# A two-layer conditioned attention kernel: in the second layer, one GpSimd chain for both normalizations, and the second film's input turned by VectorE and block loads

## The reference: what is computed

```
# layer 0
xn = layer_norm(x); q, k, v = xn @ Wq + bq, xn @ Wk + bk, (xn @ Wv + bv) * mask
y  = softmax(q k^T + mask term) v
h  = layer_norm(y) * (1 + scale(emb)) + shift(emb)         # "film"
x  = x + silu(h) @ out_w + out_b
# layer 1
xn = layernorm(x); q, k, v = ...; k = -inf and v = 0 where masked
q  = softmax(q over the 16 features); k = softmax(k over time)
y  = q @ (k^T v)                                           # linear attention per head
h  = layernorm(y) * (1 + scale(emb)) + shift(emb)
out = x + silu(h) @ film_out_W + film_out_b
```

## Time and profile before

| what | us |
|---|---|
| median of 3 runs | 890.01 (888.34 to 890.52) |
| the profiled execution, its own time | 891.08 |
| its span, first to last instruction | 889.1 |
| busy in the span: PE, DVE, ACT, POOL | 856.3, 780.8, 671.3, 615.6 |
| busy in 600 to 800 us: PE, DVE, ACT, POOL (of 200) | 200.00, 181.47, 178.34, 178.65 |

### The profile page before, as it was taken

How to read it: one execution, slowest core, us unless ns; L and a number is a source line. 1 busy time by engine, 2 the same in 40 slices (tenths; PEclk the granted TensorE clock), 3 DMA queues, 4 the chain that set the end, 5 groups by cost and what they waited for, 6 DMA issues and landing times.

```text
span 889.1 us, 23631 instructions
## 1 busy us (share of the span) xinstructions
PE 856.3 (96%) x8304; PEld 707.8 (80%) x8304; DVE 780.8 (88%) x1609; ACT 671.3 (76%) x1200; POOL 615.6 (69%) x1095
## 2 busy tenths in 40 slices
...
GB/s 257 261 191 110 176 124 166 135 147 152 139 151 146 152 128 172 114 183 118 173 116 162 99 44 113 61 83 84 85 84 84 84 84 86 95 94 90 50 31 60
DMA packets 91237, 108.55 MB, mean 122 GB/s; under 512 B 8624, under 2 KB 61328, under 8 KB 90992
## 3 DMA queue, kind: packets, MB, share of 16 engines
...
...
## 4 chain that ended last, share of the span: by engine, by line
PE 89%; DVE 3%; issue 3%; POOL 2%; ACT 1%; SPq 0%; DMA 0%; DVEq 0%; ACTq 0%; POOLq 0%
PE psX L1447 16%; PE psY L1568 13%; PE psT L1447 10%; PE psM L1447 10%; PE psT L1547 6%; PE psT L1526 5%; PE psY L1447 5%; PE psY L1593 3%; PE psM L1547 3%; PE psT L1458 3%; PE psT L1725 3%; PE psY L1678 3%; PE psM L1526 3%; PE psX L1605 2%; PE psM L1458 1%
## 5 line engine op out<-in xcount | busy, mean ns | idle before, releaser
L1037 DVE TENSOR_REDUCE sb_cm<-psT 128x4 f32<-128x1024 f32 x168 | 202.6, 1217 | 11.9 <-PE psT L1547 11.7
L618 ACT ACTIVATE sb_P<-psT 128x1024 f32<-128x1024 f32 x176 | 177.7, 1025 | 29.4 <-PE psT L1526 15.1
L1568 PE MATMUL psY<-sb_P,sb_Vp 128*17 128x256 f32 x2048 | 130.2, 383 | 1.8 <-DVE sb_yr L1063 1.2
L1037 DVE TENSOR_REDUCE sb_cm<-psM 128x4 f32<-128x1024 f32 x88 | 107.1, 1217 | 7.5 <-PE psM L1547 7.4
L418 POOL TENSOR_SCALAR sb_ve<-sb_mv 128x2 f32<-128x2 f32 x32 | 7.3, 229 | 125.0 <-DVE sb_mv L1071 124.9
L1447 PE MATMUL psX<-sb_xT,sb_W0h 128*128 128x256 f32 x488 | 93.6, 294 | 0.0
L618 ACT ACTIVATE sb_P<-psM 128x1024 f32<-128x1024 f32 x80 | 81.9, 1024 | 12.9 <-PE psM L1526 6.8
L1568 PEld LDWEIGHTS psY<-sb_P,sb_Vp 128*17 128x17 f32 x2048 | 50.3, 97 | 48.1 <-issue 5.4
L436 POOL TENSOR_TENSOR sb_qp<-sb_qp 128x512 fp32r<-128x512 f32 x64 | 82.1, 1283 | 5.3
L1547 PE MATMUL psT<-sb_Ks,sb_Qs 64*128 64x256 f32 x672 | 74.7, 304 | 2.7 <-DVE sb_cm L1037 1.4
L1526 PE MATMUL psT<-sb_Qs,sb_Ks 64*128 64x256 f32 x704 | 74.5, 296 | 2.4 <-ACT sb_P L618 2.2
...
## 6 DMA issues: line engine op xcount, KB each, us to landing
...
sb_u<-y_normed SPq DMA_DIRECT2D x128, 64.0 KB, 2.5
...
```

The lines of the kernel that those rows point to most:

```text
L618: a.activation(P[G % 4][:, :], pairs[place["S", n, g][0]][:, :], ACT.Exp).then_inc(s_ex, 1)
L1037: v.tensor_reduce(cm[n % 2][:, 4 * j:4 * j + 4], scores, AX.X, ALU.max, negate=True).then_inc(s_mx, 1)
L1568: ins = pe.matmul(psY[32 * j:32 * j + 17, y0:y0 + T], Vp[n % RING][:, m, 4 * gr + j, :], Pj[:, c0:c0 + 256], start=(m == 0), stop=(m == 1))
```

## The change

Four edits, all in the second stage:

1. `rs_pair(n)` takes the place of `rs_(n, 0)` and of `rs_(n-3, 1)` for n = 3 to 31: one chain of four instructions on four columns. It waits for the statistics of both, so for `st0_`[n] and `st1_`[n-3], and both `xn_`[n] and `yn_`[n-3] wait for it.
2. The low part of the first film's result (`hl_`) for samples 4 to 31 goes from DVE to POOL as `hl0_`, behind `xb_`.
3. For the 27 samples 0 to 26 (`BLOCKS`), `f1_` on PE is gone. A new `ynt_`[t-4] on DVE makes the 32x32 block transposes of `yn`, SyncE stores the result to a new DRAM tensor `y_second` (`fstore`) and reads it back in four block loads (`fload`), and ACT's `u_` of the second film reads that SBUF tile in the next turn, ahead of `t_`[t-5]. `o0_` no longer waits for that `u_`.
4. Order: on DVE `mq_` goes ahead of `bd_`; on ACT `hh_`[t] goes ahead of `yn_`; in the ramp `yt_`(1), (2) and (3) stand earlier.

```diff
+PAIRED = range(3, B)
+BLOCKS = B - 5
...
+        def scaled(n, l):
+            first = n if l == 0 else n + 3
+            if first in PAIRED:
+                return e_rsp, 4 * (first - 2)
+            return (e_rs0, 4 * n + 4) if l == 0 else (e_rs1, 4 * (n - B + 3) + 4)
...
+            def fstore(n):
+                sp.wait_ge(e_f1, n + 1)
+                sp.dma_start(fd[n], y1s.rearrange("p a e -> p (a e)")).then_inc(e_fd, 16)
+
+            def fload(n):
+                sp.wait_ge(e_fd, 16 * n + 16)
+                if n >= 2:
+                    sp.wait_ge(e_u1, n - 1)
+                by_block = fd[n].rearrange("(b s) (a e) -> a s b e", s=32, a=4)
+                tile = y1T[n % 2].rearrange("p b i k s -> p b (i k s)")
+                for q in range(4):
+                    sp.dma_start(tile[32 * q:32 * q + 32, :, :], by_block[q]).then_inc(e_fl[n % 2], 16)
...
                 if ok(t - 1):
                     key_mask(t - 1)
+                if 0 <= t - 4 < BLOCKS:
+                    fstore(t - 4)
+                    fload(t - 4)
...
+            def rs_pair(n):
+                done, count = scaled(n, 0)
+                g.wait_ge(e_st0, 4 * n + 4)
+                g.wait_ge(e_st1, 4 * (n - 3) + 4)
+                g.wait_ge(e_xn, n)
+                if n >= 4:
+                    g.wait_ge(e_yn, n - 3)
+                g.tensor_scalar(ve[:, :], mv[:, :, 1], EPS, None, ALU.add).then_inc(done, 1)
+                g.wait_ge(done, count - 3)
+                g.tensor_tensor(rs[:, :], ve[:, :], ph[:, :], ALU.pow).then_inc(done, 1)
+                g.wait_ge(done, count - 2)
+                g.tensor_tensor(ve[:, :], mv[:, :, 0], rs[:, :], ALU.mult).then_inc(done, 1)
+                g.wait_ge(done, count - 1)
+                g.tensor_scalar(nm[:, :], ve[:, :], -1.0, None, ALU.mult).then_inc(done, 1)
...
+            def hl0_(n):
+                g.wait_ge(e_hh0, n + 1)
...
+                g.tensor_tensor(hl[0][n % 2].bitcast(F32R), hb[0][n % 2], hh[0][n % 2], ALU.subtract).then_inc(e_hlp, 1)
...
             def yn_(n):
-                a.wait_ge(e_rs1, 4 * n + 4)
+                a.wait_ge(*scaled(n, 1))
...
+            def ynt_(n):
+
+                v.wait_ge(e_yn, n + 1)
+                if n >= 1:
+                    v.wait_ge(e_fd, 16 * n)
+                v.transpose(y1s.rearrange("p a (i k s) -> p k i a s", i=2, k=2),
+                            yn[n % 2].rearrange("p k (i a c) -> p k i a c", i=2, a=4)).then_inc(e_f1, 1)
...
                 if ok(t + 1):
                     yt_(t + 1)
+                if 0 <= t - 4 < BLOCKS:
+                    ynt_(t - 4)
                 if ok(t - 2):
                     dq_(t - 2)
+                    mq_(t - 2)
                 if ok(t - 3):
                     bd_(t - 3)
-                if ok(t - 2):
-                    mq_(t - 2)
-                if ok(t):
-                    hl_(t)
                 if ok(t - 6):
                     ob_(t - 6)
...
-                if ok(t - 4):
+                if t - 4 >= BLOCKS:
                     f1_(t - 4)
```

More of the change, by code:

```diff
@@ L192, in bass_cond_seq_kernel @@
         ub[1], th[1], hb[1], hh[1], hl[1] = ([unit() for _ in range(2)] for _ in range(5))
+        y1s = unit().rearrange("p k (b s) -> p (k b) s", k=2, b=2)
+        y1T = [unit().rearrange("p k (b i s) -> p (k b) i s", k=2, b=2, i=2)
+               .rearrange("p a i (k s) -> p a i k s", k=2) for _ in range(2)]
         R = [psT[0][:, 0:512], psT[0][:, 512:1024], psT[1][:, 0:512], psT[1][:, 512:1024],
@@ L236, in bass_cond_seq_kernel @@
         e_hlast = sem("e_hlast")
+        e_rsp, e_hlp = sem("e_rsp"), sem("e_hlp")
+        e_fd = sem("e_fd")
+        e_fl = [sem(f"e_fl{i}") for i in range(2)]
         e_xb, e_xo, e_rs0, e_rs1, e_qs = (sem(f"e_{n}") for n in ("xb", "xo", "rs0", "rs1", "qs"))
@@ L475, in rs_ @@
                 k = slice(2 * l, 2 * l + 2)
+                done, count = scaled(n, l)
                 g.wait_ge(e_st[l], 4 * n + 4)
@@ L529, in second @@
                 if ok(t - 1):
-                    rs_(t - 1, 0, e_xn)
+                    rs_pair(t - 1)
                 if ok(t):
                     xb_(t)
+                if ok(t):
+                    hl0_(t)
                 if ok(t - 2):
@@ L586, in _ @@
             kb_(B - 2)
-            rs_(B - 1, 0, e_xn)
+            rs_pair(B - 1)
             ken_(B - 2)
@@ L654, in u_ @@
             def u_(n, l, src):
-                a.wait_ge(e_f[l], n + 1)
+                if l == 1 and n < BLOCKS:
+                    a.wait_ge(e_fl[n % 2], landed(n, 2, 4))
+                else:
+                    a.wait_ge(e_f[l], n + 1)
                 if n == 0:
@@ L660, in u_ @@
                 for d in range(2):
-                    ins = a.activation(ub[l][n % 2][:, d, :], src[:, d, :], ACT.Identity,
-                                       bias=FB[:, l, d, n:n + 1], scale=FA[:, l, d, n:n + 1])
+                    dst, blocks = ub[l][n % 2][:, d, :], src[:, d, :]
+                    if l == 1 and n < BLOCKS:
+                        dst = dst.rearrange("p (k b s) -> p b k s", k=2, b=4)
+                        blocks = y1T[n % 2][:, :, d, :, :]
+                    ins = a.activation(dst, blocks, ACT.Identity, bias=FB[:, l, d, n:n + 1],
+                                       scale=FA[:, l, d, n:n + 1])
                 ins.then_inc(e_u[l], 1)
@@ L671, in xn_ @@
             def xn_(n):
-                a.wait_ge(e_rs0, 4 * n + 4)
+                a.wait_ge(*scaled(n, 0))
                 if n >= 1:
@@ L741, in second @@
                 if ok(t - 5):
+                    if t - 5 < BLOCKS:
+                        u_(t - 5, 1, r_f1)
                     t_(t - 5, 1)
```

51 lines of the change are left out of this document (26 added, 25 removed).

## The result

The changed kernel takes 909.38 us (median of 4 runs, 908.52 to 913.01) against 890.26 of before on the same chip: a ratio of 1.0239, with a 95% interval of 1.0214 to 1.0263. It is slower. The profiled execution took 909.97 us with a span of 908.2.

A forecast was written before the change was run, and what follows sets the result against it. PE's own work bounded the kernel at 10.71 us a turn; a new ring of waits would make it 11.46, +20.3 us over 27 turns. With +0.2 for the rest: 911.6 profiled, 910.5 against the median, range 894 to 922.

The forecast's parts named there:

- The ring: Second stage, once per turn: `st0_`, pair, `yn_`, `ynt_`, `dq_`, `mq_`, `bd_`, `y_`, `yd_`; summed at 11.46 us against 10.71.
- PE's wait ahead of `y_`: Sign in the changed profile: PE waits 0.7 to 1.2 us before `y_`, released by DVE's `bd_`.
- DVE's ahead of `ynt_`: Sign in the changed profile: DVE waits about 1 us before `ynt_`, released by ACT's `yn_`.
- C: Length of the paired chain on four columns on POOL: 2.22 us held, 1.87 free.
- the line through one and two columns: POOL's power took 0.57 us on one column, 0.71 on two; extended straight, 0.99 on four.
- the hold: POOL's multiply in the pair, starting beside DVE's second `h_`, is held until that ends; C 2.22 instead of 1.87.
- PE's 0.44: PE loses `f1_`, 0.44 us per turn: 10.71 to 10.27 if nothing else binds.
- The low part on POOL: `hl0_`, estimated at 1.3 us on POOL; DVE's sum stays, and any delay of `kt_` hides behind PE's slack.
- rival 2: Ring of `yn_`, `ynt_`, store, loads and ACT: summed at 10.4 us; slower DMA makes 12.0, 925 us; chance 0.13 with long power.
- The rest: Outside the steady turns: ramp -0.7 us from ACT's wait, tail +1 from `yn_`[28]; taken as +0.2 together, good to 2.
- PE before 540 us unchanged: Sign in the changed profile: PE's work ahead of 540 us, in the ramp, stays as before.

## Why the prediction was right

**The ring.** It was made from ten rows of the kernel before, and came out as predicted: 11.46 summed, 11.48 to 11.49 measured; +20.3 over 27 turns summed, +20.33 measured from `y_`[1] to `y_`[28] (the steady turns are 0.78 longer, the last of them only 0.13). PE's wait ahead of `y_` (0.92) and DVE's ahead of `ynt_` (0.92) are where they were said to be.

**C.** Summed 2.22, measured 715.09 - 712.85 = 2.24. The power on four columns takes 1.04; the line through one and two columns gave 0.99. The multiply takes 0.48, held until the end of the second `h_`; undoing the hold alone gave 0.26 a turn, so the step stands on a run and not only on an overlap in the timeline.

**PE's 0.44.** It is worth nothing here: PE waits in every turn. Nor does any version show the 10.27 in a steady turn; the shortest take 10.5. The low part on POOL was costed as neutral, since DVE's sum stays. That was the wrong reading of it. Back on DVE behind `bd_` it costs 13 us, because its place beside `qs_` holds it, so in the changed kernel it is worth 0.44 us a turn. It is also a member of the second ring, which costs 0.36 a turn once the first is gone; 0.15 of that came back when it left.

**The ring of store and loads** (rival 2) was summed at 10.4 and thought harmless. In the changed kernel it is: store to first load 2.03 us, ACT waits 0.5 us in all. The two versions with `ynt_` behind `mq_` show it at about 10.5 with late landings on top, so it stood 1 us behind, about as summed, and kept them at 892.8 and 888.7.

**The rest** was mis-sized in its terms. The ramp gained 5.3 us instead of 0.7 between the two profiles, because PE's clock stayed up there, which no row on a wait shows; this is the step that failed, and with it the sign "PE before 540 us unchanged" (PE did 342 instructions from 500 to 540 us instead of 318). Against it the first turn of the stage (+1.75) was left out and the tail cost 2.3 instead of 1. Together they give -1.2 where +0.2 was said. That they nearly cancel is luck: had the ramp been sized right and the others not, the forecast would have been 906. Part of that luck lies in the profiled execution, which had the slower clock in its ramp; against the median the ramp's order is worth 3.0 us.

**One thing the runs correct.** I put the price on the pair alone. It belongs to `ynt_` ahead of `dq_` waiting for anything that hangs on this turn's `st0_` or `h_`. The pair is one such tie: parting the chains gave 0.45 a turn with the low part on DVE. `hh_` ahead of `yn_` in ACT's list (edit 4) is another: turning the two round gave 0.58 more. How long the second tie is with the low part on POOL, as in the changed kernel, no run shows; taking from 11.48 the 0.48 by which `hl_` delays `yd_`, I estimate some 11.0, still above 10.71.
